# A four-layer graph network on one core: expansions in halves, wider stored rows, blank fills ahead of the scatter, and index copies for four chunks

## The reference

```
h = relu(layernorm(x))
x = x + L0(h, src, dst, edge_weight)   # by source: sum of edge_weight * (h @ hamilton)[dst] to src
h = relu(layernorm(x))
x = x + L1(h, src, dst)                # segment_sum((h / sqrt(deg_out) @ W)[src], dst) / sqrt(deg_in) + b
h = relu(layernorm(x))
x = x + L2(h, src, dst, edge_attr)     # segment_sum(relu(h[src] + edge_attr), dst), then two products
h = relu(layernorm(x))
x = x + L3(h, src, dst, edge_attr)     # two products with batch norms over edges, mean to src, two over nodes
```

## Time and profile before

| stage | us from the span's start |
|---|---|
| plan_edges | 4 to 133 |
| first layer_norm | 133 to 163 |
| node_product | 163 to 183 |
| scatter_by_source | 183 to 2522 |
| sums and plans up to the split of the parts | 2600 to 3140 |
| expand_by_source, layer 2 | 3140 to 3886 |
| sum_by_target, layer 2 | 3901 to 4816 |
| norm, next parts | 4816 to 4925 |
| expand_by_source, layer 3 | 4925 to 5589 |
| sum_messages_by_target | 5601 to 6365 |
| gather_by_source (last layer) | 6568 to 8766 |

### The profile page before, as it was taken

The page is one execution under the profiler, slowest core; times in us unless marked ns, Lnnn a source line. Parts: engine busy times, 40 slices in busy tenths (PEclk is TensorE's granted clock), DMA queues, the critical chain, the costliest instruction groups (busy, mean ns, idle before and its releaser), DMA issues. The chain is left out here.

```text
span 8920.1 us, 183726 instructions
## 1 busy us (share of the span) xinstructions
PE 6289.7 (71%) x35446; PEld 4927.1 (55%) x35447; DVE 5909.6 (66%) x18166; ACT 2529.7 (28%) x8033; POOL 4865.1 (55%) x4975
## 2 busy tenths in 40 slices
PE   2688888888847645556664555788668888888886
PEld 1577777777735433345553222566456666666664
DVE  8566666666669755568887888899554444444444
ACT  5355555555511222211110222111112221222222
POOL 0477777777756200047773000677347777777773
PEclk9555555555555655568886555999855555555556
DMA  6655555454546399987786999666633333333333
GB/s 133 152 154 149 156 148 154 149 156 147 156 97 139 72 190 195 195 198 224 230 226 130 246 257 257 181 181 178 92 111 82 80 80 80 81 81 80 82 80 30
DMA packets 1822628, 1295.50 MB, mean 145 GB/s; under 512 B 1262870, under 2 KB 1643574, under 8 KB 1820576
## 3 DMA queue, kind: packets, MB, share of 16 engines
q1 hardware_dynamic: 1580112, 841.10, 39.9%
q0 software_dynamic: 200704, 415.20, 17.9%
q10 hardware_dynamic: 40912, 29.67, 1.5%
HBM read 923.76 MB, written 361.78 MB: 144 GB/s over the span
## 5 line engine op out<-in xcount | busy, mean ns | idle before, releaser
L1138 POOL DMA_INDIRECT sorted_edges<-arena,idx x1664 | 1619.0, 973 | 727.8 <-issue 638.7
L2253 POOL DMA_INDIRECT arena<-node_table,idx x1760 | 1660.4, 943 | 557.0 <-issue 388.9
L1053 PE MATMUL banks<-arena,edge_tables 128*128 x3520 | 1164.7, 439 | 288.3 <-DVE edge_tables L982 233.8
L2229 PE MATMUL banks<-arena 128*128 128x64 f32 x3520 | 1214.1, 448 | 0.0
L1639 PE MATMUL banks<-arena 128*128 x3520 | 670.9, 361 | 769.2 <-issue 435.2
L1053 PEld LDWEIGHTS banks<-arena,edge_tables 128*128 128x128 f32 x3520 | 898.5, 317 | 417.6 <-issue 393.3
L2224 PE MATMUL banks<-arena 128*64 128x65 f32 x3520 | 843.0, 343 | 401.0 <-ACT arena L2240 400.3
L2128 POOL DMA_INDIRECT arena<-expanded,idx x576 | 544.6, 945 | 1003.5 <-DVE idx L2005 788.5
L2229 PEld LDWEIGHTS banks<-arena 128*128 128x128 f32 x3520 | 883.4, 311 | 210.2
L2240 ACT ACTIVATE arena<-arena 128x64 f32<-128x64 f32 x1760 | 450.1, 257 | 1787.2 <-DVE arena L2192 1781.6
L2199 DVE TENSOR_TENSOR arena<-arena,banks 128x64 f32 x1760 | 387.8, 220 | 820.2 <-PE banks L2229 792.8
(11 more groups left out here) (426 smaller groups left out, 11712.5 us busy)
## 6 DMA issues: line engine op xcount, KB each, us to landing
arena<-sorted_edges SPq DMA_DIRECT2D x220, 524.0 KB
arena<-lanes_dram SPq DMA_DIRECT2D x222, 512.0 KB, 8.0
expanded<-arena SPq DMA_DIRECT2D x110, 784.0 KB, 8.0
arena<-in_attr_rows SPq DMA_DIRECT2D x576, 130.0 KB
arena<-sorted_edges SPq DMA_DIRECT2D x110, 536.0 KB
arena<-row_keys SPq DMA_DIRECT2D x110, 512.0 KB
arena<-sorted_edges SPq DMA_DIRECT2D x110, 512.0 KB, 5.6
expanded<-arena SPq DMA_DIRECT2D x110, 512.0 KB
```

The costliest lines, as they stand in the source:

```text
L1053: nc.tensor.matmul(m.psum[j % 4][:, 0:D], m.onehot[:, j % 4, :], m.support[:, bass.ds(blocks[j] * D, D)], start=True, stop=True).then_inc( ...
L1138: nc.gpsimd.indirect_dma_start(m.sorted, bass.IndirectOffsetOnAxis(ap=m.idx[:, j % (4 * CH):j % (4 * CH) + 1], axis=0), m.out_ring[:, slot ...
L2229: nc.tensor.matmul(m.psum[j % 4][:, 0:D], m.onehot8[:, c % 4, j % CB, :], row[:, 0:D], start=True, stop=True).then_inc(s["summed"], 1)
L2253: nc.gpsimd.indirect_dma_start(slots[:, j % SLOTS, 0:D], None, m.table, bass.IndirectOffsetOnAxis(ap=m.idx[:, j % SLOTS:j % SLOTS + 1], ax ...
```

## The change

Four things are changed.

- *Expansions by halves.* A chunk is taken out in two halves of eight tiles (four banks) in place of four quarters. In layer 2 ACT alone copies the rows, in two instructions of 128 x 8 x 192 a chunk; DVE keeps `turn`, `reach` and `take`; ACT waits for `take` of the chunk before, and one semaphore `put` replaces `put_act` and `put_dve`. PE loads the chunk's 16 block numbers at once. In layer 3 DVE makes six additions of 512 elements in place of twelve of 256, and ACT two ReLUs in place of four.
- *The stored row of layer 2* is 112 words (448 B) in place of 98 (392 B). The target number stays in word 97; words 98 to 111 are zeros, written once.
- *The blank fills* are written by one function, `fill_blanks`. The blank record on chip is two records wide, so a fill is one run of 390 floats per partition in place of two of 195. Blocks 0 to 23 are filled by SP in the first `layer_norm`, 24 to 97 by ACT where all stood before.
- *The index copies* in both sums by target are made for four chunks at once (128 x 16) at every fourth chunk.

Some small buffers move to other places (`wide_tiles`, `less`, `onehot_attr`), to make room.

The diff, cut to its core:

```diff
-ROW2 = PARTS // 2 + 2
+ROW2 = 112
+COUNT2 = PARTS // 2
+DST2 = COUNT2 + 1
...
-    m.blank_record = sb("blank_record", [P, REC])
+    m.blank_record = sb("blank_record", [P, 2 * REC])
...
+FILLED_EARLY = 24
+
+
+def fill_blanks(nc, engine, kind, m, lo, hi):
+
+    pairs = m.sorted.rearrange("(p t) f -> p (t f)", p=P)
+    for b in range(lo, hi):
+        if b % 8 == 0:
+            last = run_values(nc, kind, m.last_tile[0:1, b:min(b + 8, hi)], TS - 1)
+        engine.dma_start(pairs[:, bass.ds(last[b % 8] * REC, 2 * REC)], m.blank_record[:, :]).then_inc(m.filled, 16)
+
+
+def layer_norm(nc, m, degrees=None, table=None, copy=None, fills=0):
...
+        if fills:
+            @block.sync
+            def _(sp):
+                fill_blanks(nc, sp, ENG.SP, m, 0, fills)
...
-            for b in range(NB):
-                if b % 8 == 0:
-                    last = run_values(nc, ENG.Activation, m.last_tile[0:1, b:min(b + 8, NB)], TS - 1)
-                act.dma_start(sorted_tiles[:, bass.ds(last[b % 8], 2), :], m.blank_record[:, :].unsqueeze(1).to_broadcast([P, 2, REC])).then_inc(s["filled"], 16)
+            act.wait_ge(m.filled, 16 * FILLED_EARLY)
+            fill_blanks(nc, act, ENG.Activation, m, FILLED_EARLY, NB)
...
-            pool.wait_ge(s["filled"], 16 * NB)
+            pool.wait_ge(m.filled, 16 * NB)
...
+                v.memset(out16[:, :, :, PARTS + 4:2 * ROW2].rearrange("p c t f -> p (c t) f"), 0.0).then_inc(s["blank"], 1)
...
-            def take(i, c, u):
+            def take(i, c, h):
                 n = i * chunks + c
-                v.tensor_reduce(m.found[:, bass.ds(n * SET + u // 2 * (SET // 2), SET // 2)],
-                                quad[:, 2 * u + 1, FOUND:FOUND + 3 * (SET // 2)].rearrange("p (e n) -> p e n", n=3), AX, ALU.add
+                dve.wait_ge(s["expanded"], n * 2 + h + 1 + 2 * 2)
+                v.tensor_reduce(m.found[:, bass.ds(n * SET + h * (SET // 2), SET // 2)],
+                                quad[:, 4 * h + 3, FOUND:FOUND + 3 * (SET // 2)].rearrange("p (e n) -> p e n", n=3), AX, ALU.add
                                 ).then_inc(s["taken"], 1)
 
-            def put(i, c, u):
-                n = i * chunks + c
-                dve.wait_ge(s["expanded"], n * 4 + u + 1 + 2 * 4)
-                to = rows_of(out16, c, u)[:, :, :, 0:PARTS]
-                v.tensor_copy(to, quad[:, 2 * u:2 * u + 2, 0:2 * PARTS].rearrange("p k (t f) -> p k t f", f=PARTS)).then_inc(s["put_dve"], 1)
-                take(i, c, u)
-
-            def add(i, c, u):
-                n = i * chunks + c
-                k = n * 4 + u
-                dve.wait_ge(s["expanded"], k + 1 + 2 * 4)
-                if u == 0:
+            def add(i, c, h):
+                k = (i * chunks + c) * 2 + h
+                dve.wait_ge(s["expanded"], k + 1 + 2 * 2)
+                if h == 0:
                     dve.wait_ge(attr_in[c % 5], i * (chunks // 5 * 16) + c // 5 * 16 + 16)
-                to, attr = rows_of(out, c, u), rows_of(m.attr_rows, c, u)
-                v.tensor_tensor(to, sum_of(u, 0), attr, ALU.add).then_inc(s["summed"], 1)
+                to, attr = half_of(out, c, h), half_of(m.attr_rows, c, h)
+                v.tensor_tensor(to, sum_of(h, 0), attr, ALU.add).then_inc(s["summed"], 1)
                 dve.wait_ge(s["summed"], 2 * k + 1)
-                v.tensor_tensor(to, to, sum_of(u, 1), ALU.add).then_inc(s["summed"], 1)
+                v.tensor_tensor(to, to, sum_of(h, 1), ALU.add).then_inc(s["summed"], 1)
                 dve.wait_ge(s["summed"], 2 * k + 2)
-                v.tensor_tensor(to, to, sum_of(u, 2), ALU.add).then_inc(s["added"], 1)
+                v.tensor_tensor(to, to, sum_of(h, 2), ALU.add).then_inc(s["added"], 1)
...
-                    if not first or c >= 5:
+                    if layer == 3 and (not first or c >= 5):
                         dve.wait_ge(stored[c % 5], i * (chunks // 5 * 16) + c // 5 * 16)
-                    for u in range(4):
+                    for h in range(2):
                         if layer == 3:
-                            add(i, c, u)
-                        elif u % 2:
-                            put(i, c, u)
+                            add(i, c, h)
+                        else:
+                            take(i, c, h)
...
+                    numbers = run_values(nc, ENG.PE, m.sorted_block[:, bass.ds(n * SB, SB)], NB)
                     pe.wait_ge(s["turned"], n + 1)
-                    for u in range(4):
-                        k = n * 4 + u
-                        if u % 2 == 0:
-                            numbers = run_values(nc, ENG.PE, m.sorted_block[:, bass.ds(n * SB + 4 * u, 8)], NB)
-
+                    for h in range(2):
                         if layer == 3:
-                            pe.wait_ge(s["added"], k + 1)
-                        elif u % 2:
-                            pe.wait_ge(s["put_dve"], n * 2 + u // 2 + 1)
-                            pe.wait_ge(s["taken"], n * 2 + u // 2 + 1)
+                            pe.wait_ge(s["added"], n * 2 + h + 1)
                         else:
-                            pe.wait_ge(s["put_act"], n * 2 + u // 2 + 1)
+                            pe.wait_ge(s["put"], n * 2 + h + 1)
+                            pe.wait_ge(s["taken"], n * 2 + h + 1)
                         settle(pe)
-                        for j in range(4):
-                            done = nc.tensor.matmul(quad[:, 2 * u + j // 2, j % 2 * PARTS:(j % 2 + 1) * PARTS],
-                                                    m.turned16[:, c % 2, (4 * u + j) * P:(4 * u + j + 1) * P],
-                                                    parts[:, bass.ds(numbers[4 * (u % 2) + j] * PARTS, PARTS)], start=True, stop=True)
-                        if layer == 2 and u % 2:
+                        for j in range(HALF):
+                            t = HALF * h + j
+                            done = nc.tensor.matmul(quad[:, t // 2, t % 2 * PARTS:(t % 2 + 1) * PARTS],
+                                                    m.turned16[:, c % 2, t * P:(t + 1) * P],
+                                                    parts[:, bass.ds(numbers[t] * PARTS, PARTS)], start=True, stop=True)
+                        if layer == 2:
                             for e in range(SET // 2):
-                                g = u // 2 * (SET // 2) + e
+                                g = h * (SET // 2) + e
                                 if e == 0:
                                     pe.wait_ge(s["reached"], n * SET + g + SET // 2)
-                                done = nc.tensor.matmul(quad[:, 2 * u + 1, FOUND + 3 * e:FOUND + 3 * e + 3],
+                                done = nc.tensor.matmul(quad[:, 4 * h + 3, FOUND + 3 * e:FOUND + 3 * e + 3],
...
-                    for u in range(4):
+                    for h in range(2):
                         if layer == 3:
-                            act.wait_ge(s["added"], n * 4 + u + 1 + 4)
-                            rows = out[:, c % 5, 4 * u:4 * u + 4, :]
+                            act.wait_ge(s["added"], n * 2 + h + 1 + 2)
+                            rows = out[:, c % 5, HALF * h:HALF * h + HALF, :]
                             a.activation(rows, rows, ACT.Relu).then_inc(s["row"], 1)
-                        elif u % 2 == 0:
-                            act.wait_ge(s["expanded"], n * 4 + u + 1 + 2 * 4)
-                            a.activation(rows_of(out16, c, u)[:, :, :, 0:PARTS],
-                                         quad[:, 2 * u:2 * u + 2, 0:2 * PARTS].rearrange("p k (t f) -> p k t f", f=PARTS),
-                                         ACT.Copy).then_inc(s["put_act"], 1)
-
-            act.sem_inc(s["put_act"], 2)
+                        else:
+                            act.wait_ge(s["expanded"], n * 2 + h + 1 + 2 * 2)
+                            act.wait_ge(s["taken"], n * 2 + h + 1 + 2)
+                            a.activation(half_of(out16, c, h)[:, :, :, 0:PARTS],
+                                         quad[:, 4 * h:4 * h + 4, 0:2 * PARTS].rearrange("p k (t f) -> p k t f", f=PARTS),
+                                         ACT.Copy).then_inc(s["put"], 1)
+
+            if layer == 2:
+                act.wait_ge(s["blank"], 2)
+                act.sem_inc(s["put"], 2)
...
-        aims = 8
-        aimed = lambda c: slice(c % aims * groups, c % aims * groups + groups)
-        assert BODY_D % deep == 0 and BODY_D % aims == 0
+        aims = 2 * AIM
+        aimed = lambda c: slice(c % aims * groups, c % aims * groups + AIM * groups)
...
-                v.tensor_copy(m.idx[:, aimed(c)], m.granule[:, bass.ds(n * groups, groups)]).then_inc(s["aimed"], 1)
+                v.tensor_copy(m.idx[:, aimed(c)], m.granule[:, bass.ds(n * groups, AIM * groups)]).then_inc(s["aimed"], 1)
...
-                    aim(n + AIM, c + AIM)
+                    if c % AIM == 0:
+                        aim(n + AIM, c + AIM)
...
```

(29 more changed lines are left out.)

53 lines of the change are left out of this document (26 added, 27 removed).

## The result

Four runs of the changed kernel took 8730.66 to 8742.4 us, median 8735.11; four of the kernel before 8924.55 to 8934.04, median 8932.7. The ratio is 0.9781, with a 95% interval of 0.9765 to 0.9798. The profiled execution took 8731.67 us with a span of 8729.9, 190.2 less than before.

What follows compares the result with a forecast made beforehand. Bounds: PE's two loads per chunk in the layer-2 expansion, transfers close behind; transfers in layer 3; PE's wait behind the fills. Terms -152 - 40 - 2 - 14 + 7 + 2 = -199 give 8724, predicted 8735 us, range 8655 to 8910.

Steps and rivals of the forecast that it cites:

- The second-layer expansion: Layer-2 expansion: one load of numbers, halves and cheaper row packets cut a chunk from 6.78 to 5.4 us, -152 us.
- always stretched as SP's lane issue stretches it: Layer-2 expansion, upper end: PE's new load is lengthened by 1.11 us like the slow one, chunk 6.27 us.
- beginnings at multiples of 64 B: Layer-2 stored rows: those beginning at multiples of 64 B escape a surcharge, so 448-B packets cost 29.2 ns, not 46.9.
- The equal surcharge of 18 to 20 ns: Layer-2 rows of 392 B and blank fills of 780 B: both cost 18 to 20 ns a packet above the line.
- The fills: Blank fills before the scatter: 24 moved to SP and wider records save 40 us, capped by PE's 47.9 us wait.
- The third-layer expansion: Layer-3 expansion: transfers bind, so DVE's saved 0.98 us a chunk becomes waiting for lane rows; -2 us in all.
- The index copies: Both sums by target: 108 of 144 copies go in each, -9 us in layer 3 and -5 in layer 2.
- The wider gather: Layer-2 sum by target: rows read grow by 14%, DVE's wait for edge rows by 7%, +7 us.
- The rows stay dear: Rival, layer-2 expansion: 448-B packets cost 49.6 ns, transfers bind at 7.08 us a chunk, total 8920 us; chance 0.19.
- The load stays slow: Rival, layer-2 expansion: PE's load stays stretched, chunk 6.27 us, -56 in place of -152, total 8830 us; chance 0.08.
- In the third layer SP never paused: Sign against the rival that the layer-3 expansion follows DVE: a further -106 us, total 8630 us; chance 0.06.
- the 8909: Total in us if packets are priced by beats, 17 for 448 B against 16.4 for 392 B; weighed with "The rows stay dear".

Runs made afterwards that it cites:

- the first group: Follow-up runs with other widths of the stored layer-2 row, in the changed kernel or the kernel before; the kernel before took 8921.6 us beside them.
- the row alone: The kernel before with layer-2 rows of 112 words in place of 98 and nothing else changed: 8957.7 us, ratio 1.0033.
- the second group: Follow-up runs on index copies, loads of block numbers and early fills, on a chip slower by 1%; the kernel before took 9018.1 us there.

## Why the prediction was right, point by point

It was right in sum, 8735 us for 8735.11, and nearer there than in its terms. That it came so near is luck: the terms miss by up to 13 us, both ways.

*The second-layer expansion* (-152, measured -163). Each of its two bounds was read from the profile and is there: PE's two loads now, the transfers close behind. The load's floor of 1.10 us came out as predicted (1102 ns at the shortest), and the choice of 5.4 us between 5.16 and 6.27 stood close to 5.33, but by another road: the load is 0.4 us longer than its floor while SP issues nothing beside it, so "always stretched as SP's lane issue stretches it" was not what the load's length hangs on. The price of a 448-B packet (29.2 predicted, 27.4 measured by the same reckoning) was right, and the reason for it, beginnings at multiples of 64 B, was wrong: the runs fit 32. For rows of 416 B the expectation drawn from that reason had no gain from the row, where there is one. The equal surcharge of 18 to 20 ns that the prediction saw on 392 and 780 B is one of its reckoning, which left the lane rows' packets at 206 ns; by their own durations 392-B packets paid 11 to 12 ns more than 448-B ones. The edit to halves was given nothing of its own, and the runs put about 0.9 us a chunk on it with ACT's evacuation. Two errors cancel there: of the 5.16 us the gap was to be 1.52 and PE's own work the old 3.64, and they are 1.99 and 3.24.

*The fills* (-40, measured -45): the cap of 47.9 us was reached. What was mis-sized is the run on ACT: 74 x 0.76 + 21 = 77 us were predicted, 64 measured (0.86 a fill, SP's loads included). The 21 us for SP's loads beside it are what was too large: with no early fills, 24 more cost 82.43 - 63.99 = 18.4 us, or 0.77 each as forecast, and 74 of those leave 7 us of the 64.

*The third-layer expansion* (-2, measured -3.5): nothing, as said. In the first group it took 676.8 us by quarters (the row alone) and 675.9 and 675.7 by halves. DVE's wait for lane rows rose by (83.5 - 25.0) / 66 = 0.89 us a chunk, where 0.9 was expected.

*The index copies* (-14): this step failed. The copies by themselves change nothing (0.9998). The prediction took a stretch without a pause beside one copy for the whole stage. DVE does wait for PE there, and what it saves it waits: in the layer-3 sum 83.8 and 8.4 us before (the first just ahead of the copy), and 62.8, 29.9 and 17.8 after:

```profile
DVE idx L2005 <- PE banks L2042: 83.8, 56, 8.0
...
DVE arena L2025 <- PE banks L2042: 8.4, 9, 1.9
```

```profile
DVE arena L2025 <- PE banks L2051: 62.8, 50, 4.2
...
DVE idx L2015 <- PE banks L2051: 29.9, 19, 8.3
...
DVE arena L2034 <- PE banks L2051: 17.8, 13, 2.8
```

*The wider gather* (+7): too small. With 98 words the sum takes 951.6 and 952.3 us, with 104 or 112 of them 963.8 to 976.1 on chips of the same speed: +12 to +24. On the slower chip of the second group the difference doesn't show (974.5 with 98 words, 969.9 to 981.0 with 112), so its size is not settled. DVE's wait for edge rows grew from 119.5 to 146.8 us over the stage, though the rows themselves have not changed.

The errors of the terms (-11, -5, -2 one way, some +22 in the two sums the other) and 7 us by which the medians differ more than the profiled executions make up most of the rest.

*The rivals.* "The rows stay dear" is what 392 B show (700.7 us for the stage), and did not occur, since 448 B are seven times 64 and so also fourteen times 32. "The load stays slow" was half true: 1.49 us, neither 1.10 nor 2.2. In the third layer SP never paused. (The 16.4 beats that the prediction estimates by the Trainium skill, "DMA: Bandwidth & Descriptors", How a descriptor splits into AXI transactions, for 392 B come out as 16.5 over the places where such rows can begin, which moves the 8909 there by some 5 us.)

## What to carry to other kernels

Where two bounds lie a few per cent apart, an edit that lifts one gains little or nothing and the two together gain all: price them together, and test each alone. Look at what a stored row does to 32-B pieces before choosing its width; padding that raises the bytes by 14% lowered the mean time of a stored packet from 38.8 to 27.7 ns in a full queue. Work that is hidden under an idle queue's cover is free only up to the end of that cover, and worth no more than the wait that it removes.

## What was not expected of the hardware

Stores of rows of 392 or 400 B took 39 to 40 and 36 ns a packet on the mean, of 416 or 448 B 26 to 28, with medians of 24 to 27 ns for all of them. A register load of 16 numbers on PE took 1.10 to 1.67 us in the changed kernel's layer-2 expansion, and what makes the difference stays open: SP issued nothing beside it, and with half of DVE's work taken away it was longer, 1.58 us.
